# First expert layer: gate and up products as three fp32r products of split operands

## The reference

```
scores = softmax(x @ gate_w.T)                      # x: 1024 x 256, 16 experts
topk_w, topk_idx = top_k(scores, 2)
gu = einsum('th,ehj->etj', x, w_gate_up)            # 256 -> 2 * 176 per expert
h  = silu(gu[..., :176]) * gu[..., 176:]
y  = einsum('eti,eih,te->th', h, w_down, combine)   # 176 -> 256
y += (silu(g_s) * u_s) @ shared_down                # shared expert, 256 -> 2 * 352 -> 256
```

## Time and profile before

| | us |
|---|---|
| timed executions | 730.10, 730.45, 732.13 (median 730.45) |
| the profiled execution | 723.44 |
| its span, first to last instruction | 721.6 |
| TensorE busy (PE) | 659.8 (91%) |
| VectorE busy (DVE) | 405.8 (56%) |
| ScalarE busy (ACT) | 340.2 (47%) |
| GpSimd busy (POOL) | 309.3 (43%) |
| mean granted TensorE clock | 0.969 |

### The profile page before, as it was taken

How to read it: one execution, slowest core, us unless ns; L and a number is a source line. 1 busy time by engine, 2 the same in 40 slices (tenths; PEclk the granted TensorE clock), 3 DMA queues, 4 the chain that set the end, 5 groups by cost and what they waited for, 6 DMA issues and landing times. The chain is left out here.

```text
span 721.6 us, 12441 instructions
## 1 busy us (share of the span) xinstructions
PE 659.8 (91%) x4222; PEld 553.4 (77%) x4222; DVE 405.8 (56%) x1063; ACT 340.2 (47%) x836; POOL 309.3 (43%) x377
## 2 busy tenths in 40 slices
PE   3888999999999999999999997889999968996997
PEld 3767888988988979979979896776666556986754
DVE  6758487196295295494493646783222269555343
ACT  2655766567467567566566561323343321200221
POOL 4565462552453444353351111616666315200563
PEclk9999999999999999999999999799999979995999
DMA  8011010110210200200100131993233162009440
GB/s 263 30 41 49 30 32 30 55 36 7 64 32 2 65 29 0 65 29 12 55 1 1 42 78 65 334 368 95 92 94 90 52 216 80 1 29 365 135 121 23
DMA packets 29778, 57.90 MB, mean 80 GB/s; under 512 B 4670, under 2 KB 15904, under 8 KB 29728
## 3 DMA queue, kind: packets, MB, share of 16 engines
q1 hardware_dynamic: 22720, 42.03, 17.1%
q0 software_dynamic: 4896, 13.12, 6.2%
q10 hardware_dynamic: 2112, 2.10, 0.8%
HBM read 48.06 MB, written 10.09 MB: 81 GB/s over the span
## 5 line engine op out<-in xcount | busy, mean ns | idle before, releaser
L911 DVE RECIPROCAL denominators<-readings 128x2 f32<-128x2 f32 x128 | 21.2, 166 | 147.6 <-PE readings L587 146.9
L447 POOL TENSOR_TENSOR w_high<-xn,ones 128x256 fp32r<-128x256 f32 x84 | 53.9, 672 | 76.7 <-PE ahead L235 35.5
L587 PEld LDWEIGHTS readings<-memory_copy,sigma 128*128 128x128 f32 x512 | 75.2, 191 | 11.2 <-ACT memory_copy L784 2.2
L793 ACT ACTIVATE memory_reading<-readings,denominators 64x128 f32<-64x128 f32 x256 | 78.7, 357 | 6.0 <-DVE denominators L911 4.0
L587 PE MATMUL readings<-memory_copy,sigma 128*128 128x129 f32 x512 | 78.8, 276 | 2.2 <-ACT memory_copy L784 2.1
L784 ACT ACTIVATE memory_copy<-memory 128x258 f32<-128x258 f32 x128 | 50.2, 392 | 61.9 <-PE memory L597 47.9
L917 DVE SCALAR_TENSOR_TENSOR minus_delta<-readings,denominators,v 64x128 f32<-64x128 f32 x240 | 73.8, 347 | 4.5 <-DVE denominators L911 0.3
L597 PE MATMUL memory<-minus_delta,sigma_k_tokens 128*128 128x129 f32 x480 | 73.2, 275 | 0.0
L1221 POOL DMA_INDIRECT xs_e<-rows_e,gather_at_e x46 | 44.6, 969 | 54.3 <-DVE gather_at_e L1635 19.0
L1368 PE MATMUL up_e<-weights_e,xT_e 128*128 x184 | 66.4, 483 | 1.2 <-ACT xT_e L1497 1.2
L451 POOL TENSOR_TENSOR w_low<-xn,w_high 128x256 fp32r<-128x256 f32 x84 | 65.7, 813 | 1.6
(11 more groups left out here) (282 smaller groups left out, 1444.6 us busy)
## 6 DMA issues: line engine op xcount, KB each, us to landing
weights_e<-experts SPq DMA_DIRECT2D x24, 608.0 KB, 12.1
xn<-L_attn_Wq SPq DMA_DIRECT2D x8, 512.0 KB, 3.9
xn<-L_attn_Wk SPq DMA_DIRECT2D x7, 512.0 KB, 3.8
xn<-L_attn_Wv SPq DMA_DIRECT2D x7, 512.0 KB, 3.8
wo<-L_attn_Wo SPq DMA_DIRECT2D x1, 2048.0 KB, 13.2
rows_e<-xn ACTq DMA_DIRECT2D x4, 512.0 KB, 10.4
x<-L_attn_x SPq DMA_DIRECT2D x4, 256.0 KB, 3.4
x<-L_attn_x SPq DMA_DIRECT2D x2, 512.0 KB, 3.5
```

What stands on the lines that cost most here:

```text
L447: last = pool.tensor_tensor(w_high[i][:, :, of], w_stage[:, :, of], one, ALU.mult)
L587: last = pe.matmul(KQ[g][:, hh * MC:(hh + 1) * MC], sqk[:, GROUP * g + hh, pair, 2 * par:2 * par + 2, :], mz[g][:, hh, :], start=True, sto ...
L793: last = act.activation(read[rows, half, GROUP * g + hh, pair, :], KQ[g][rows, hh * MC:hh * MC + DK], ACT.Copy, scale=nr[g][rows, hh:hh + 1])
```

## The change

The first mixture's blocks take their gate and up products in three fp32r products, as the shared expert does. Four things change.

Weights: `split_high(b)` on ScalarE copies the 704 columns of a block's gate and up weights as fp32r into `block_high[b % 2]`, `split_low(b)` on VectorE subtracts that from the weights into `block_low[b % 2]`. Their space is `w_high` and `w_low` of the shared tiles 0 and 1. Each is done for `b + 2` in step `b`, for blocks 0 and 1 ahead of the loop. Both engines read the place of the weights from `weight_at` themselves.

Rows: `xT` is fp32r now, and `rows_low(b)` on VectorE subtracts it from XT into `xT_low`, which lies in h_high[1]; in the listings below TensorE's third product therefore reads h_high_e.

Products: `block_gate_up` has six fp32r matmuls of 352 columns (L233 to L235) instead of two fp32 ones, and their addresses are fixed. It waits for `xt_low_done` and `block_split`; `turn_rows` waits for `xt_low_done` instead of `xt_copied`.

Order ahead of the loop: `down(3)` stands before `gate_up(4)` now, since it is the last reader of the tiles that the blocks' weights overwrite, and VectorE subtracts weights and rows before it adds the shared result.

```diff
@@ set up
+        if shared:
+            xT = [sb(f"xT{i}", [P, KD, P], F32R) for i in range(2)]
+            xT_low = [h_high[1][:, i * D:(i + 1) * D].rearrange("p (k c) -> p k c", k=KD) for i in range(2)]
+            block_high, block_low = ([a[i][:, :, :].rearrange("p i n -> p (i n)")[:, 0:4 * INTER] for i in range(2)]
+                                     for a in (w_high, w_low))
@@ TensorE
             def block_gate_up(b, first):
-                pe.wait_ge(xt_copied, b + 1)
+                if shared:
+                    pe.wait_ge(xt_low_done, b + 1)
+                    pe.wait_ge(block_split, b + 1)
...
+                        last = split3(pe, GU[b % 2][:, 0:2 * INTER], (xT[b % 2][:, k, :], xT_low[b % 2][:, k, :]),
+                                      (block_high[b % 2][:, at], block_low[b % 2][:, at]), k == 0, k == KD - 1)
...
                 number_slots()
+                down(3)
                 gate_up(4)
-                down(3)
@@ ScalarE
+            def split_high(b):
+                if b == 1:
+                    act.wait_ge(down_done, 4)
+                elif b >= 2:
+                    act.wait_ge(gu_ready, b - 1)
+                first = act.value_load(weight_at[b:b + 1, 0:1], min_val=0, max_val=(E - 1) * WIDE)
+                act.activation(block_high[b % 2], flat[:, bass.ds(first, 4 * INTER)], ACT.Copy)\
+                   .then_inc(block_high_done, 1)
+            if shared:
+                act.wait_ge(weights_loaded, 16 * E)
+                act.wait_ge(experts_ready, 1)
+                split_high(0)
+                split_high(1)
...
                     copy_rows(b + 2)
+                    if shared:
+                        split_high(b + 2)
@@ VectorE
+            def rows_low(b):
+                dve.wait_ge(xt_copied, b + 1)
+                dve.tensor_tensor(xT_low[b % 2], XT[b % 2][:, 0:D].rearrange("p (k c) -> p k c", k=KD),
+                                  fr(xT[b % 2][:, :, :]), ALU.subtract).then_inc(xt_low_done, 1)
+            def split_low(b):
+                first = dve.value_load(weight_at[b:b + 1, 0:1], min_val=0, max_val=(E - 1) * WIDE)
+                dve.wait_ge(block_high_done, b + 1)
+                dve.tensor_tensor(block_low[b % 2], flat[:, bass.ds(first, 4 * INTER)], fr(block_high[b % 2]),
+                                  ALU.subtract).then_inc(block_split, 1)
...
                 hidden_low(4)
+                split_low(0)
+                split_low(1)
+                dve.wait_ge(down_done, 4)
+                rows_low(0)
                 add_shared(1, LAST - 1)
+                rows_low(1)
                 add_shared(0, LAST)
...
                     copy_hidden(b - 1)
+                if shared and b + 2 < NB:
+                    rows_low(b + 2)
+                    split_low(b + 2)
```

More of the change, by code:

```diff
@@ L1093, in sparse_layer @@
         xs = [sb(f"xs{i}", [P, ROW]) for i in range(RING)]
-        xT = [sb(f"xT{i}", [P, KD, P]) for i in range(2)]
+        if shared:
[3 more added lines that the diff above has]
+                                     for a in (w_high, w_low))
+            xt_low_done, block_high_done, block_split = sem("xt_low_done"), sem("block_high_done"), sem("block_split")
+        else:
+            xT = [sb(f"xT{i}", [P, KD, P]) for i in range(2)]
         gated = [sb(f"gated{i}", [P, INTER]) for i in range(2)]
@@ L1356, in turn_rows @@
                 else:
-                    pe.wait_ge(xt_copied, b - 1)
+                    pe.wait_ge(xt_low_done if shared else xt_copied, b - 1)
                 for k in range(KD):
@@ L1363, in block_gate_up @@
             def block_gate_up(b, first):
-                pe.wait_ge(xt_copied, b + 1)
+                if shared:
+                    pe.wait_ge(xt_low_done, b + 1)
+                    pe.wait_ge(block_split, b + 1)
+                else:
+                    pe.wait_ge(xt_copied, b + 1)
                 if b >= 2:
@@ L1367, in block_gate_up @@
                 for k in range(KD):
-                    last = pe.matmul(GU[b % 2][:, 0:2 * INTER], xT[b % 2][:, k, :],
-                                     flat[:, bass.ds(first + k * 2 * INTER, 2 * INTER)],
-                                     start=k == 0, stop=k == KD - 1)
+                    if shared:
+                        at = slice(k * 2 * INTER, (k + 1) * 2 * INTER)
+                        last = split3(pe, GU[b % 2][:, 0:2 * INTER], (xT[b % 2][:, k, :], xT_low[b % 2][:, k, :]),
+                                      (block_high[b % 2][:, at], block_low[b % 2][:, at]), k == 0, k == KD - 1)
+                    else:
+                        last = pe.matmul(GU[b % 2][:, 0:2 * INTER], xT[b % 2][:, k, :],
+                                         flat[:, bass.ds(first + k * 2 * INTER, 2 * INTER)],
+                                         start=k == 0, stop=k == KD - 1)
                 last.then_inc(gu_ready, 1)
```

## The result

Beside each other on one chip, the changed kernel took 734.6 us (median of 12 runs, 730.1 to 740.9) and the kernel before 730.3 (12 runs, 726.6 to 733.1): ratio 1.0061, 95% interval 1.0037 to 1.0085. It is slower by 0.6%, where 727.0 and faster was forecast. The profiled execution took 736.18 us, its span is 734.4.

A forecast was written before the change was run, and what follows sets the result against it. TensorE's own work was taken to bound the first layer's block loop. A start 2.8 us later less 6.4 saved, taken as -3.4, gave 720.0 profiled; 7.0 added gave 727.0 us, range 724.0 to 734.5.

The forecast's parts named there:

- TensorE, one block: Block loop: six fp32r matmuls take 1.06 us instead of 1.29, saving 0.23; period 2.65 instead of 2.88.
- ScalarE, VectorE: Block loop: weight copy 0.80 us, subtraction 0.88; cycles 2.2 and 2.3 us, both under the 2.65 period.
- Rival 1: Block loop: VectorE becomes the bound through its register read, cycle 2.93 us; +4.2, 734.7 us; chance 0.16.
- GpSimd: Block loop: gather and scatter allow a 2.56 us period; nothing added for VectorE's new subtraction beside them.
- Rival 4: Block loop: GpSimd stands still during VectorE's weight subtraction, cycle 3.44 us; +18.5, 749 us; chance 0.05.
- The start: Loop start: new order and splits delay the first gate and up step 1.5 us, the fourth 2.8.
- 492.5 + 1.29 + 0.26 + 0.8 + 0.88: Loop start: VectorE's work ahead of the third step, from shared-result addition to block 2's weights, summed to 495.55.
- Rival 2: Loop start: the clock falls to half over the first steps, +2.2; in all -1.2, 729.2 us; chance 0.17.
- The sum: Whole kernel: 2.8 lost at the start less 6.4 saved is -3.6, taken as -3.4 us.
- The step that failed: Whole kernel: the shown runs' median lies 7.0 us above the profiled execution; added to 720.0, giving 727.0.
- 28 steps (3 to 30) save 0.23 each: 6.4 us: Block loop: from the fourth step TensorE has more to do than VectorE, so each shorter step's saving counts.
- my four rivals: VectorE as bound, 0.16; clock falling, 0.17; cheaper start or timely fp32r weights, 0.12; GpSimd held up, 0.05.

The follow-up runs named there:

- 9: Changed kernel with the first layer's scatters moved behind the block loop: 764.7 us, those scatters included; 25 blocks 66.67 us.
- 10: Kernel before with the first layer's scatters moved behind the block loop: 768.6 us, those scatters included; 25 blocks 71.94 us.
- 15: Changed kernel a third time, nothing changed in it: 721.0 us against 724.1 for the kernel before, ratio 0.9966.
- the first trace of before: First profiled execution of the unchanged kernel before, which the forecast rests on: 723.44 us; 25 blocks 71.94 us.
- 12: Changed kernel with first-layer scatters of 64 rows instead of 128, all rows sent again behind the loop: 760.3 us, and 759.0 when repeated.
- 13: Changed kernel with the first layer's scatters replaced by plain SyncE stores: 722.1 us, ratio 0.9991, and 720.4 us when repeated.
- first trace: First profiled execution of the changed kernel, nothing else altered: 736.18 us; 25 blocks 76.20 us.
- 1: Changed kernel again, nothing changed in it: 737.6 us against 733.6 for the kernel before, ratio 1.0041.
- 8: Changed kernel with VectorE's subtraction for the weights' low parts replaced by a copy of one input: ratio 1.0033 to the kernel before.
- experiment 4: Kernel before traced again, nothing changed in it: profiled execution 735.28 us, group median 733.6 us; 25 blocks 79.07 us.
- 3: Changed kernel with gate and up products in fp32 from unsplit weights, keeping splits, waits and new order: 738.8 us, ratio 1.0072 to the kernel before.
- 2: Kernel before with only the new order, the last shared down products ahead of the last gate and up products: ratio 1.0008.
- 7: Kernel before with SyncE adding eight updates of an unused semaphore in each block: ratio 0.9996.
- 11: Kernel before with each down product of 256 columns made as two of 128: ratio 1.0022.
- 5: Changed kernel with blocks 0 and 1 in fp32 from unsplit weights and the old order: 737.4 us against 732.3 for the kernel before, ratio 1.0064.
- 6: Changed kernel with 25 useless transposes added where TensorE waits at the loop's start: ratio 1.0017 to the kernel before.

## Why the prediction was wrong, step by step

- *TensorE, one block: right.* 1.07 us for 1.06, period 2.66 to 2.67 for 2.65, 5.27 us gained in 25 blocks (experiments 9 and 10; 15 against the first trace of before).
- *ScalarE, VectorE: right.* 0.79 and 0.89 us for 0.80 and 0.88. Rival 1 is refuted: TensorE is busy in all 66.67 us of 15.
- *GpSimd: right in the result, wrong in the reason.* I took nothing for the subtraction, from a row in which the gather had started first. A transfer that starts within a subtraction is held, but only for what is left of it, and only about every second one starts there. Rival 4's 3.44 us don't come.
- *The start: right at full clock, too small below it.* With the clock at 1.00 (12, whose start is that of the changed kernel) it is 18.58 us against 15.95: +2.6 at the sixth transposes, where one step of 0.22 is already saved; I had 2.8 at the fourth step, and there it is 17.51 against 14.67. Partly this is luck: 492.5 + 1.29 + 0.26 + 0.8 + 0.88 in the prediction is 495.73 and not 495.55, and the first step came 1.9 us late, not 1.5. The clock adds to it: 0.9 us at 0.91 (9, 13, 15) and 2.4 at 0.76 (first trace, 1). Rival 2 held in six of the seven traces of the table with this start (first, 1, 8, 9, 13, 15; not 12), and cost more than the +2.2 I gave it where the half clock lasted 10.24 us.
- *The sum, in a group without late steps: the right way, and smaller.* 15 to its fourth step is +3.7 (18.36 against 14.67), the next 27 steps -5.7 (71.78 against 77.47): -2.0 us; measured -2.5 (0.0034 x 724.1; -3.1 by the medians), between the forecast and rival 2.
- *The step that failed* is the sentence "The runs shown have a median of 730.45, 7.0 above the profiled execution; I put the same difference on it", and with it the term "28 steps (3 to 30) save 0.23 each: 6.4 us", which it carried over to those runs. The 7.0 us are no constant beside the kernel. They are late steps, in just these loops: 25 blocks of the first and the second layer cost the kernel before 7.1 and 5.6 us more in experiment 4 than in the trace that I had read; and in the groups without late steps the median of the kernel before is 723.4 and 724.1, with nothing to add. Where late steps occur, the 6.4 us are not there: by the medians of experiments 1 and 3 the shorter products gave 1.3 us, and the waits, splits and order cost 5.2 instead of 2.8, which makes the +3.9 us measured in that group (+4.3 in the first).

The traces of these groups point the same way, less surely. The five with a 2.88 or 2.90 us period (2, 3, 4, 7, 11) take 73.8 to 79.1 us for 25 blocks, mean 75.6, and the five with 2.67 us (the first of the changed kernel, 1, 5, 6, 8) 74.7 to 78.7, mean 76.2: nothing is left to see of the 5.3 us, within some 3 us. The start costs 5.0 us more by the two first traces, 2.6 to 4.1 against the starts of 16.9 to 18.4 us that the old order has elsewhere. That the start is the whole of the +3.9 and +4.3 us isn't shown, and experiment 5 speaks against it: its start is as short as before's, and it is 5.1 us slower.

So none of my four rivals was the cause. The missing one was: something outside the trace that I read already limits the loop in most runs, and there TensorE's own work is not all that counts.

*What stays open.* Which property of the scatters does it (software queue, completions, bytes): the two kernels that were to tell met no late steps in either try. Whether it is the chip: late steps were met on chips 8 (twice) and 4, none on 0, 11 and 15, and no chip showed both, so chip and late steps can't be told apart. Whether late steps would be there without a recording: they come with missing records, and I have no run without any. And why 5, whose start was good, had 1.0064 in its group; its 25 blocks of 78.7 us are the longest of this period, but one trace can't say that its twelve runs were like it.

## What to carry to other kernels

A profiled execution that is 1% faster than the median of the runs is not the same case as they are: before an offset is put on a forecast, ask for a second trace, and compare a stage that the change doesn't touch (here the second layer, 35.7 or 41 us). A gain per step counts only if the engine that was made faster is the bound in the runs that are measured. Work that is prepared ahead costs its latency once at the loop's start; leaving the first two blocks unprepared won all of that back here once (15.87 us at a clock of 1.00) and once 1.9 us of it (17.53 against 19.43, at 0.90 and 0.91).

## What the runs showed of the hardware

- Of 27 indirect transfers of GpSimd that start within VectorE's subtraction of two SBUF inputs (experiment 15), 26 are held and end 0.84 to 0.88 us after it; one that has started before runs its usual 0.97. A copy of one SBUF input (experiment 8) held six gathers too.
- TensorE's signals can be seen up to 3 us late by those who wait for them, while its matmuls go on at their pitch, and then several come at once (527 us in the first trace, 536 us in experiment 4). In four groups of runs this occurred in each trace, in every loop that scatters and gathers; in three (chips 0, 11 and 15) it did not, with the same code. The kernel before takes 730.0 to 733.6 us in the ones and 723.4, 724.1 and (one run) 720.8 in the others.
- fp32r products of 352 columns start 0.16 us apart at full clock; the first behind an fp32 matmul of 48 rows takes 0.27. A register read lies beside the running instruction of ScalarE and left it idle for 0.24 to 0.25 us; VectorE, with the same read, is idle ahead of its subtraction only in its wait for ScalarE's copy (0.58 us at 504.46).
